# Attention phase: the finished batch's four tiles normalised on GpSimd, the new batch's four on ScalarE, one in a slot

## The chip, the cores and the metric

The kernel runs on one core of one Trainium2 chip. The time is the device time of one launch, in microseconds, median of several runs. The kernel is a whole two-layer network in one program of 39,953 instructions. The engines have queues of their own and are tied together by semaphores: TensorE (PE: matmuls and transposes, its weight loads shown as PEld), VectorE (DVE), ScalarE (ACT), GpSimd (POOL) and SyncE (SP, the DMAs).

## What is computed

The input is 16 batches of 512 rows of 128 numbers. The reference is a chain of six residual blocks; the change lies in the phase that computes the first three and prepares the fourth:

```python
x = x + 0.5 * L0_ffn(layernorm(x))     # sqrt((xn @ cos(..))**2 + (xn @ sin(..))**2)
x = x + L0_attn(layernorm(x))          # 16 heads, rotary, softmax(q k * scale) v, Wo
x = x + 0.5 * L0_ffn(layernorm(x))
x = x + 0.5 * L1_ffn(layernorm(x))     # top-2 counts of 8 experts over all rows
x = x + L1_attn(layernorm(x))          # a state-space mixer in chunks of 128
x = x + 0.5 * L1_ffn(layernorm(x))
```

`layernorm(x)` is `(x - mean) / sqrt(var + 1e-5)` over the 128 numbers of a row. The kernel computes it as `x * rstd + shift` with `shift = -mean * rstd`, one `rstd` and one `shift` for each row, so for each partition of a tile of 128 rows.

## The kernel before

**Three phases.** `attention_phase` runs first, to about 1617 us, then `mixer_phase` and `last_ffn_phase`. Each phase has its own semaphores and ends in a `sem_clear` on GpSimd and a barrier.

**Iterations and slots.** The attention phase has 19 iterations (`ITERATIONS = BATCH + 3`), and each has 64 slots (`SLOTS = NT * HEADS`). A slot is a place in the order in which each engine's queue is written: every engine's block has the loop `for i ... for q in range(SLOTS)`, and the table `ATTENTION_AT` says at which slot which step is issued. Within an engine, instructions run strictly in that order. Iteration i works on three batches at once: it takes in the *new* batch i (`is_new`, i up to 15), does attention for batch i - 2 (`is_att`, i from 2 to 17) and finishes the *old* batch i - 3 (`is_old`, i from 3). So iterations 3 to 15 have a new and an old batch ("mixed"), 0 to 2 only a new one, 16 to 18 only an old one; 18 has no attention.

**The attention inside a slot.** For each slot TensorE issues one matmul of shifted scores (`shifted_scores`, L708), which ScalarE turns into exponentials (`exponentials`, L506), and one matmul of plain scores for the next batch (`scores`, L724), of which VectorE takes the maximum (L347). The shifted scores go to one of two banks and wait for the exponential two before. Once in four slots TensorE issues `values` (L746), and once in eight `denominators` (L755). The latter read `prs`, the sums of two heads' exponentials, which GpSimd makes in `add_pair` (L579), four for each pair: those of heads 6 and 7 at slots 28 to 31, and the denominators that read them at slot 35. Exponentials of the next head but one overwrite the exponentials that were summed, and so wait for `prs` too (slots 32 to 35 for the pair of slots 28 to 31).

**The two laps.** Beside this, each iteration norms its tiles twice. Tiles 0 to 3 of `xn` belong to the new batch, 4 to 7 to the old one. Lap 1 (before the feed-forward block): statistics on VectorE at slots 5 and 6, aggregation at slot 8; `reciprocal_deviations` on GpSimd at slot 8 (L563 the power, L566 the shift); `normalise` on ScalarE at slots 11 to 14 (L468), a quarter of the iteration's tiles in each: two in a mixed iteration, one otherwise; `transposes` on TensorE at slot 16 (L634), the evacuation on ScalarE at 17 (L457), the feed-forward matmuls at 18 and 22 (L650), squares (L478) and their sums on GpSimd (L571), the root at 25 (L543), the residual on VectorE at 25 and 26 (L320). Lap 2 (before attention for the new batch, before the gate for the old one): statistics at 27 and 28, aggregation and deviations at 29, `normalise` at 31 to 34, transposes at 36, evacuation at 35 (behind the exponential of that slot), gate at 37 (L659), projections from 37 on (L665).

**Order on GpSimd in lap 2.** At slot 28 one sum of the pair, at slot 29 L563 and L566, then the sum of slot 29, then those of 30 and 31. The sums of slots 29 to 31 stand in the queue behind the deviations.

ScalarE's normalisation before:

```python
act.wait_ge(S["shift"], 2 * i + lap)
ts = tiles(i)
for t in ts[len(ts) // 4 * part:len(ts) // 4 * (part + 1)]:
    ins = a.activation(xn[:, t, :], src(t), ACT.Identity, scale=rstd[:, t:t + 1],
                       bias=shift[:, t:t + 1])
```

TensorE's transposes wait for one semaphore `xn`, which the last tile's normalisation raises. SyncE's queue (the loads of the next batch, the stacked queries and keys, the stores of the old batch) has no step at the edited place: its DMAs wait for `y_new`, `y_old`, `lo`, `st` and `mrow`.

Of the kernel before, what the change touches and what calls it, by code (L numbers as in the profile page):

```python
# [18 lines left out]
ALU = mybir.AluOpType  # L19
ACT = mybir.ActivationFunctionType  # L20
# [4 lines left out]
NT = SEQ // P  # L25
# [4 lines left out]
STK = 3 * DH + 1  # L30
W_SCALE = 64.0
ATT_SCALE = float((64 / 16) ** -0.5)


def rope_tables():
# [48 lines left out]
def attention_phase(nc, ins, x3_out, n3_out, w, cnt_acc, later):  # L84
# [4 lines left out]
    with ExitStack() as ctx:  # L89
        def sb(name, shape, dt=F32):  # L90
            return ctx.enter_context(nc.sbuf_tensor(name, shape, dt))

        x8 = sb("x8", [P, 8, D])
# [36 lines left out]

        ps = ctx.enter_context(nc.psum_tensor("ps", [P, 8, 512], F32))

        names = ("x_in", "var", "xn", "xT", "xnT", "ff", "sq", "ss", "h", "y_new", "y_old", "pair", "pair_free",
                 "rot", "hi", "lo", "gate", "gate_read", "st", "exp", "s", "s_read", "mrow", "rstd",
                 "pv", "den", "norm", "wo", "x2", "v", "dve", "x_out", "ones",
                 "xnh", "xnl", "v_ps", "prs", "dn", "dd", "o", "shift", "place_in", "n_out", "kept_hi", "kept_lo",
# [4 lines left out]
        for c in range(HEAD_GROUPS):  # L141
            S["stacked", c] = ctx.enter_context(nc.semaphore(f"a_stacked{c}"))
        nums = sorted(s.num for s in S.values())
        assert nums[-1] - nums[0] + 1 == len(nums)


        first, second = (pr[:, k].rearrange("p t n -> p (t n)") for k in range(2))
# [26 lines left out]
        def is_new(i):  # L174
            return i < BATCH
# [4 lines left out]
        def is_old(i):  # L180
            return 3 <= i
# [4 lines left out]
        def tiles(i):  # L186
            return [NT * h + t for h in halves(i) for t in range(NT)]
# [25 lines left out]
        with nc.Block(no_gpsimd_drain=True) as block:  # L213
# [234 lines left out]
            def _(act):  # L448
# [12 lines left out]
                            act.wait_ge(S["v_ps"], NT * (i - 1))  # L461
                        a.copy(xnh[:, i % 2], ps[:, 4, :]).then_inc(S["xnh"], 1)

                def normalise(i, src, lap, part):
                    act.wait_ge(S["shift"], 2 * i + lap)
                    ts = tiles(i)
                    for t in ts[len(ts) // 4 * part:len(ts) // 4 * (part + 1)]:
                        ins = a.activation(xn[:, t, :], src(t), ACT.Identity, scale=rstd[:, t:t + 1],  # L468
                                           bias=shift[:, t:t + 1])
                        if t == ts[-1]:  # L470
                            ins.then_inc(S["xn"], 1)

                def squares(i, k):
                    f = ffns_before(i) + k
# [36 lines left out]
                for i in range(ITERATIONS):  # L511
                    for q in range(SLOTS):
                        s, g = q // NG, q % NG
                        if is_att(i):
                            exponentials(i - 2, s, g)
                            if q in AT["values"]:
                                t = AT["values"].index(q)
                                act.wait_ge(S["v_ps"], NT * (i - 2) + t + 1)
                                a.copy(vt[:, t, :], ps[:, 5, :]).then_inc(S["v"], 1)
                            if s and s % NG == 0 and g == 3:  # L520
                                numerators(i - 2, s // NG - 1)
                        for part in range(4):
                            if q == AT["xn1"] + part:
                                normalise(i, lambda t: x8[:, t, :], 1, part)
                            if q == AT["xn2"] + part:
                                if part == 0:
                                    if is_new(i):
                                        act.wait_ge(S["y_new"], i + 1)
                                    if is_old(i):
                                        act.wait_ge(S["y_old"], i - 2)  # L530
                                normalise(i, lambda t: ynew[:, i % 4, t, :] if t < NT else yold[:, t - NT, :], 2, part)
                        if q == AT["evac1"]:
                            transposed(i, 1)
                        if q == AT["squares"]:
                            for k in range(2):
                                squares(i, k)
                        if q == AT["squares_b"]:
                            for k in range(2, len(tiles(i)) // 2):
                                squares(i, k)
                        if q == AT["sqrt"]:  # L540
                            a0, b0 = span(i)
                            act.wait_ge(S["ss"], ffns_before(i + 1))
                            a.activation(hh[:, a0:b0, :], hh[:, a0:b0, :], ACT.Sqrt, scale=0.25).then_inc(S["h"], 1)  # L543
                        if q == AT["evac2"]:
                            transposed(i, 2)
                        if is_old(i) and q == AT["next_hi"]:
                            act.wait_ge(S["xnT"], 2 * i + 2)
                            if i > 3:
                                act.wait_ge(S["n_out"], 16 * (i - 3))
                            a.copy(kept[:, 0], xnTo[:, :]).then_inc(S["kept_hi"], 1)  # L550
                        if is_new(i) and q in high_at:
                            high(i, high_at[q])
                    if is_att(i):
                        numerators(i - 2, NG - 1)

            @block.gpsimd
            def _(pool):
                g = nc.gpsimd

                def reciprocal_deviations(i, lap):  # L560
# [4 lines left out]
                    pool.wait_ge(S["rstd"], 2 * i + lap)  # L565
                    g.tensor_tensor(shift[:, a0:b0], nmean[:, a0:b0], rstd[:, a0:b0], ALU.mult).then_inc(S["shift"], 1)  # L566

                def add_squares(i, k):
                    pool.wait_ge(S["sq"], ffns_before(i) + k + 1)
                    t = tiles(i)[2 * k]  # L570
                    g.tensor_tensor(hh[:, t:t + 2, :], sq[:, k % 2, :, 0, :], sq[:, k % 2, :, 1, :],  # L571
                                    ALU.add).then_inc(S["ss"], 1)
# [19 lines left out]
                for i in range(ITERATIONS):  # L592
                    for q in range(SLOTS):
                        if q == AT["aggr1"]:
                            reciprocal_deviations(i, 1)
                        if q == AT["squares"]:
                            for k in range(2):
                                add_squares(i, k)
# [2 lines left out]
                                add_squares(i, k)  # L601
                        if q == AT["aggr2"]:
                            reciprocal_deviations(i, 2)
                        if is_old(i) and q == AT["next_lo"]:
                            pool.wait_ge(S["kept_hi"], i - 2)
                            g.tensor_tensor(kept[:, 1], xnTo[:, :], kept[:, 0], ALU.subtract).then_inc(S["kept_lo"], 1)
# [13 lines left out]
            def _(pe):  # L620
                mm = nc.tensor.matmul

                def transposes(i, lap):
                    pe.wait_ge(S["xn"], 2 * i + lap)
                    if lap == 1:
                        if is_att(i):
                            pe.wait_ge(S["v"], NT * (i - 1))
# [141 lines left out]
                for i in range(ITERATIONS):  # L769
# [33 lines left out]
                    if is_att(i):  # L803
                        values(i - 2, NG * NT - 1)
                        denominators_directly(i - 2, HEADS - 1)
        nc.gpsimd.sem_clear(range(nums[0], nums[-1] + 1))
        nc.all_engine_barrier(sem_only=True)


# [132 lines left out]
def mixer_phase(nc, x_in, n_in, x_out, n_out, w, ew, cnt_acc):  # L942
# [4 lines left out]
    with ExitStack() as ctx:  # L947
# [60 lines left out]
               "sqy": NT, "ms_mm": NT, "ms": 1, "rms": 1}  # L1008
        S = {n: ctx.enter_context(nc.semaphore("m_" + n)) for n in [*PER, "x_in0", "x_in1", "x_out0", "x_out1", "n_in0", "n_in1", "n_out", "dve", "pool", "start", "counted", "weights", "rate"]}
        nums = sorted(s.num for s in S.values())  # L1010
        assert nums[-1] - nums[0] + 1 == len(nums)

        AT = MIXER_AT
        SLOTS = 1 + max(max(a) if isinstance(a, tuple) else a for a in AT.values())
# [14 lines left out]
        with nc.Block(no_gpsimd_drain=True) as block:  # L1029
# [493 lines left out]
            def _(pe):  # L1523
# [144 lines left out]
                for i in range(ITERATIONS):  # L1668
                    ffn, prep, scan, tail = batches(i)
                    for q in range(SLOTS):  # L1670
# [55 lines left out]
                        if prep is not None:  # L1726
# [7 lines left out]
                                turn_bc(prep)  # L1734
                            if q == AT["scores"]:
                                scores(prep)
        nc.gpsimd.sem_clear(range(nums[0], nums[-1] + 1))
        nc.all_engine_barrier(sem_only=True)


def last_ffn_phase(nc, x_in, n_in, x_out, w, ew, cnt_acc):
# [4 lines left out]
    with ExitStack() as ctx:  # L1746
# [17 lines left out]
        for k in range(OUT):  # L1764
            S["x_out", k] = ctx.enter_context(nc.semaphore(f"f_x_out{k}"))
        nums = sorted(s.num for s in S.values())
        assert nums[-1] - nums[0] + 1 == len(nums)

        def upto(name, b, n):

# [5 lines left out]
        with nc.Block(no_gpsimd_drain=True) as block:  # L1776
# [139 lines left out]
            def _(pe):  # L1916
# [24 lines left out]
                for b in range(BATCH + 1):  # L1941
                    for e in range(EXPERTS):
                        if b < BATCH:
                            expert(b, e)
                        if e == 7 and b:
                            turn_sum(b - 1)
        nc.gpsimd.sem_clear(range(nums[0], nums[-1] + 1))
        nc.all_engine_barrier(sem_only=True)


# [45 lines left out]
```

## Time and profile before

| | |
|---|---|
| median of 3 runs | 2524.42 us |
| the runs | 2524.15, 2524.42, 2532.09 us |
| profiled execution: span | 2524.8 us |
| attention phase | to about 1617 us |
| iterations 3 to 15 | 229.06 to 1450.93 us |
| PE busy | 2163.5 us (86%) |
| DVE busy | 1827.8 us (72%) |
| POOL busy | 1455.5 us (58%) |
| ACT busy | 1410.7 us (56%) |

The span runs from the first instruction's start to the last one's end in the profiled execution; no time outside it is listed for that execution, so its own time is taken as the span of 2524.8 us, which is 0.4 us above the median. A row of a timeline has the start and the duration in us, the engine, the line, the operation, out<-in by the program's names, shapes, the number of instructions taken together, and in brackets how long the engine stood idle before it and what it waited for. `PEclk` is the share of full speed that TensorE's clock was granted.

### The profile page before, as it was taken

What the parts mean: (1) busy time and instruction counts of PE and PEld (TensorE: products, weight loads), DVE (VectorE), ACT (ScalarE), POOL (GpSimd) and SP (SyncE); (2) the same over time, 40 slices, a digit from 0 to 9 for tenths busy, and PEclk for the clock granted to TensorE, in tenths of its full rate; (3) what the DMA queues carried; (4) which work ended last, traced back from release to release, by engine and by line L of the source; (5) the groups of instructions that cost most, each with busy time, mean ns of one, the idle gap of its engine ahead of it and who ended that gap; (6) DMA issues with size and microseconds to landing.
All of it is one profiled execution on the core that took longest, in us unless ns stands there. A gap on an engine that the chain in (4) does not pass through costs nothing. (4 is left out here: it accounts for less than half of the span.)

```text
span 2524.8 us, 39953 instructions
## 1 busy us (share of the span) xinstructions
PE 2163.5 (86%) x14226; PEld 994.3 (39%) x14226; DVE 1827.8 (72%) x4240; ACT 1410.7 (56%) x2651; POOL 1455.5 (58%) x1264
## 2 busy tenths in 40 slices
PE   3689989989889889989989998569898899898878
PEld 1223333333323333323323322236566566665534
DVE  5777777777777777777777773358888888887668
ACT  2166566566566566566566566254555655556234
POOL 3366666665665665665665645146555656565358
PEclk9799999999999999999999999689999999999789
DMA  3221211112112112112112120100000000000033
GB/s 116 55 49 38 50 36 46 47 35 51 42 34 51 43 34 56 38 34 58 35 34 59 31 69 9 30 13 22 26 22 26 26 22 26 22 18 14 14 100 109
DMA packets 86598, 103.70 MB, mean 41 GB/s; under 512 B 10240, under 2 KB 68736, under 8 KB 86272
## 3 DMA queue, kind: packets, MB, share of 16 engines
q1 hardware_dynamic: 86400, 101.16, 15.3%
q8 instruction: 113, 1.85, 0.3%
q14 instruction: 85, 0.70, 0.1%
HBM read 29.55 MB, written 20.97 MB: 20 GB/s over the span
## 5 line engine op out<-in xcount | busy, mean ns | idle before, releaser
L347 DVE TENSOR_REDUCE mS<-ps 128x1 f32<-128x512 f32 x1024 | 676.9, 681 | 301.8 <-PE ps L724 297.3
L506 ACT ACTIVATE pr<-ps 128x512 f32<-128x512 f32 x1024 | 585.9, 597 | 383.7 <-PE ps L708 365.6
L579 POOL TENSOR_TENSOR prs<-pr 128x512 f32<-128x512 f32 x384 | 487.3, 1288 | 243.3 <-ACT pr L506 243.3
L708 PE MATMUL ps<-qst,kst 97*128 97x512 f16 x1024 | 397.2, 391 | 53.3 <-ACT pr L506 52.2
L724 PE MATMUL ps<-kst,qst 96*128 96x512 f16 x1024 | 400.4, 392 | 36.6 <-DVE mS L347 25.7
L746 PE MATMUL ps<-pr,vt 128*32 128x512 f32 x2048 | 279.6, 619 | 0.0
L708 PEld LDWEIGHTS ps<-qst,kst 97*128 97x128 f16 x1024 | 99.1, 98 | 419.3 <-ACT pr L506 307.3
L583 POOL TENSOR_TENSOR terms<-terms 128x512 f32<-128x512 f32 x128 | 162.4, 1268 | 69.3 <-DVE terms L340 69.3
L340 DVE TENSOR_TENSOR terms<-ps,shared 128x512 f32<-128x512 f32 x256 | 173.1, 678 | 34.9 <-POOL lo L588 29.7
L588 POOL TENSOR_TENSOR lo<-terms,hi 128x512 f16<-128x512 f32 x128 | 148.0, 1156 | 76.9 <-ACT hi L486 76.9
L724 PEld LDWEIGHTS ps<-kst,qst 96*128 96x128 f16 x1024 | 101.1, 99 | 150.4 <-DVE mS L347 80.1
L486 ACT CAST hi<-terms 128x512 f16<-128x512 f32 x128 | 78.8, 616 | 114.0 <-POOL terms L583 114.0
L755 PE MATMUL ps<-prs,ones 128*32 128x512 f32 x768 | 108.2, 637 | 33.9 <-POOL prs L579 33.9
L1394 ACT ACTIVATE m_sqy<-m_yzT 128x256 f32<-128x256 f32 x64 | 26.6, 415 | 179.3 <-DVE m_yzT L1205 179.2
L665 PE MATMUL ps<-xnh,wq 128*128 128x512 f16 x256 | 98.9, 390 | 31.3 <-DVE terms L340 22.4
L1491 POOL TENSOR_TENSOR m_own<-m_own 128x256 f32<-128x256 f32 x64 | 78.1, 1221 | 78.9 <-ACT m_own L1372 78.9
L1164 DVE TENSOR_TENSOR m_xv<-m_xr,m_coef 128x1536 f32<-128x1536 f32 x64 | 118.5, 1854 | 0.0
L1533 PE MATMUL m_ps<-m_xe,ew_hl 128*128 128x512 f16 x384 | 105.3, 395 | 9.8 <-DVE ew_hl L1240 4.2
L1486 POOL TENSOR_TENSOR m_rl<-m_rl 128x512 f32<-128x512 f32 x32 | 60.3, 1886 | 91.5 <-ACT m_rl L1398 91.5
L563 POOL TENSOR_TENSOR rstd<-veps,minus_half 128x8 f32<-128x8 f32 (+1 forms) x38 | 55.1, 1450 | 96.2 <-DVE veps L313 96.2
L665 PE MATMUL ps<-xnh,wk 128*128 128x512 f16 x256 | 97.2, 382 | 12.4 <-DVE terms L340 12.4
L571 POOL TENSOR_TENSOR xn<-sq 128x256 f32<-128x256 f32 x64 | 46.7, 749 | 100.4 <-ACT sq L478 100.3
(267 smaller groups left out, 4399.2 us busy)
## 6 DMA issues: line engine op xcount, KB each, us to landing
qst<-hi SPq DMA_DIRECT2D x128, 128.0 KB, 2.4
kst<-hi SPq DMA_DIRECT2D x128, 128.0 KB, 2.4
qst<-lo SPq DMA_DIRECT2D x64, 128.0 KB, 2.4
kst<-lo SPq DMA_DIRECT2D x64, 128.0 KB, 2.4
x<-in_q SPq DMA_DIRECT2D x16, 256.0 KB, 2.8
shared<-in_rope SPq DMA_DIRECT2D x1, 4096.0 KB, 14.4
x<-yold SPq DMA_DIRECT2D x16, 256.0 KB, 2.5
n<-kept SPq DMA_DIRECT2D x16, 256.0 KB, 2.1
```

Source lines behind the costliest of these rows:

```text
L340: v.tensor_tensor(terms[:, p % 2, c, :], ps[:, 4 + c, :], w["rope"][:, 2 * kq + c, g, :], ALU.mult).then_inc(S["pair_free"], 1)
L347: v.tensor_reduce(mS[:, b % 2, t, s:s + 1], ps[:, 2 + n % 2, :], AX, ALU.max).then_inc(S["s_read"], 1)
L506: a.activation(pr[:, s % 2, g, :], ps[:, g % 2, :], ACT.Exp, scale=ATT_SCALE).then_inc(S["exp"], 1)
L579: g.tensor_tensor(prs[:, c, :], pr[:, 0, c, :], pr[:, 1, c, :], ALU.add).then_inc(S["prs"], 1)
L583: g.tensor_tensor(terms[:, p % 2, 0, :], terms[:, p % 2, 0, :], terms[:, p % 2, 1, :], ALU.add).then_inc(S["rot"], 1)
L588: g.tensor_tensor(lo[:, p // NG, p % NG, :], terms[:, p % 2, 0, :], hi[:, p // NG, p % NG, :], ALU.subtract).then_inc(S["lo"], 1)
L665: ins = mm(out, lhs[a], rhs[b], start=k == 0, stop=k == 2)
L708: mm(ps[:, g % 2, :], kst[:, h, P * kt:P * kt + P], qst[:, h, :], start=True, stop=True).then_inc(S["st"], 1)
L724: mm(ps[:, 2 + n % 2, :], qst[0:3 * DH, h, P * t:P * t + P], kst[0:3 * DH, h, :], start=True, stop=True).then_inc(S["s"], 1)
L746: ins = mm(ps[DH * g:DH * g + DH, 6, :], vt[:, kt, DH * h:DH * h + DH], pr[:, s % 2, g, :], start=kt == 0, stop=kt == NT - 1, skip_group_c ...
L755: ins = mm(ps[DH * g:DH * g + DH, 7, :], w["ones"][:, 0:DH], prs[:, g, :], start=n % 2 == 0, stop=n % 2 == 1, skip_group_check=True)
L1164: v.tensor_tensor(xv[:, t % 2].rearrange("p c h r q -> p c h (r q)"), xr[:, b % 2, t].rearrange("p (o h) r q -> p o h (r q)", o=1).to_broa ...
```

## The change

The old batch's four tiles are normalised by GpSimd, at slot 8 for lap 1 and at slot 29 for lap 2, right behind the deviations. Each is one `tensor_scalar` with a multiplication and an addition, with two scalars for each partition; GpSimd waits first for its own shift to be complete. ScalarE keeps the new batch's four, one in each of slots 11 to 14 and 31 to 34, and nothing in iterations 16 to 18. A new semaphore `xn_old` counts GpSimd's part, and TensorE's transposes wait for `xn`, `xn_old` or both. Semaphore numbers need no longer be contiguous; at the end of each phase they are cleared in as many ranges as there are. In the new iterations 0 to 2 ScalarE's work is as before.

```diff
+def clear_semaphores(nc, nums):
+    first = nums[0]
+    for n, after in zip(nums, nums[1:] + [None]):
+        if after != n + 1:
+            nc.gpsimd.sem_clear(range(first, n + 1))
+            first = after
...
-                def normalise(i, src, lap, part):
+                def normalise(i, src, lap, t):
                     act.wait_ge(S["shift"], 2 * i + lap)
-                    ts = tiles(i)
-                    for t in ts[len(ts) // 4 * part:len(ts) // 4 * (part + 1)]:
-                        ins = a.activation(xn[:, t, :], src(t), ACT.Identity, scale=rstd[:, t:t + 1],
-                                           bias=shift[:, t:t + 1])
-                        if t == ts[-1]:
-                            ins.then_inc(S["xn"], 1)
+                    ins = a.activation(xn[:, t, :], src, ACT.Identity, scale=rstd[:, t:t + 1],
+                                       bias=shift[:, t:t + 1])
+                    if t == NT - 1:
+                        ins.then_inc(S["xn"], 1)
...
-                        for part in range(4):
-                            if q == AT["xn1"] + part:
-                                normalise(i, lambda t: x8[:, t, :], 1, part)
-                            if q == AT["xn2"] + part:
-                                if part == 0:
-                                    if is_new(i):
-                                        act.wait_ge(S["y_new"], i + 1)
-                                    if is_old(i):
-                                        act.wait_ge(S["y_old"], i - 2)
-                                normalise(i, lambda t: ynew[:, i % 4, t, :] if t < NT else yold[:, t - NT, :], 2, part)
+                        for t in range(NT):
+                            if is_new(i) and q == AT["xn1"] + t:
+                                normalise(i, x8[:, t, :], 1, t)
+                            if is_new(i) and q == AT["xn2"] + t:
+                                act.wait_ge(S["y_new"], i + 1)
+                                normalise(i, ynew[:, i % 4, t, :], 2, t)
...
+                def normalise_old(i, lap):
+                    b = i - 3
+                    if lap == 1:
+                        pool.wait_ge(S["xT"], 2 * i)
+                    else:
+                        pool.wait_ge(S["y_old"], b + 1)
+                    pool.wait_ge(S["shift"], 2 * i + lap)
+                    for t in range(NT, 2 * NT):
+                        src = x8[:, t, :] if lap == 1 else yold[:, t - NT, :]
+                        ins = g.tensor_scalar(xn[:, t, :], src, rstd[:, t:t + 1], shift[:, t:t + 1], ALU.mult, ALU.add)
+                    ins.then_inc(S["xn_old"], 1)
...
                         if q == AT["aggr1"]:
                             reciprocal_deviations(i, 1)
+                            if is_old(i):
+                                normalise_old(i, 1)
...
                         if q == AT["aggr2"]:
                             reciprocal_deviations(i, 2)
+                            if is_old(i):
+                                normalise_old(i, 2)
...
                 def transposes(i, lap):
-                    pe.wait_ge(S["xn"], 2 * i + lap)
+                    if is_new(i):
+                        pe.wait_ge(S["xn"], 2 * i + lap)
+                    if is_old(i):
+                        pe.wait_ge(S["xn_old"], 2 * (i - 3) + lap)
...
-        nc.gpsimd.sem_clear(range(nums[0], nums[-1] + 1))
+        clear_semaphores(nc, nums)
```

## Rows read from the trace of the kernel before

**Rows 1.** The page: busy time and share of the span, by engine.

```profile
PE 2163.5 (86%) x14226; PEld 994.3 (39%) x14226; DVE 1827.8 (72%) x4240; ACT 1410.7 (56%) x2651; POOL 1455.5 (58%) x1264
```

**Rows 2.** Iterations 3 to 15: us, busy (x) of PE, PEld, DVE, ACT, POOL; clock, DMA.

```profile
229.06:1450.93 1221.87, 1100.05 (x6188) 393.18 (x6188) 894.31 (x1995) 763.89 (x1417) 760.77 (x651) 0.98 0.18 43
```

**Rows 3.** Timeline of POOL: the deviations of lap 1, iterations 3, 9, 10, 16.

```profile
229.06 1.65 POOL L563 TENSOR_TENSOR rstd<-veps,minus_half 128x8 f32<-128x8 f32 x1 [0.88 <-DVE veps L313]
...
792.75 1.65 POOL L563 TENSOR_TENSOR rstd<-veps,minus_half 128x8 f32<-128x8 f32 x1 [0.87 <-DVE veps L313]
...
887.50 1.65 POOL L563 TENSOR_TENSOR rstd<-veps,minus_half 128x8 f32<-128x8 f32 x1 [0.88 <-DVE veps L313]
...
1450.93 1.02 POOL L563 TENSOR_TENSOR rstd<-veps,minus_half 128x4 f32<-128x4 f32 x1 [0.18 <-DVE veps L313]
```

**Rows 4.** Waits of PE in iterations 3 to 15: us, times, longest.

```profile
PE ps L708 <- ACT pr L506: 47.9, 78, 1.0
PE ps L755 <- POOL prs L579: 26.9, 38, 1.0
```

**Rows 5.** Timeline of ACT, iteration 8, lap 1: slots 11, 15 and 16.

```profile
701.57 0.88 ACT L468 ACTIVATE xn<-x,shift,rstd 128x128 f32<-128x128 f32 x2 [0.30 <-POOL shift L566]
...
706.09 1.06 ACT L506 ACTIVATE pr<-ps 128x512 f32<-128x512 f32 x2
```

**Rows 6.** Timeline of PE, iteration 8, lap 1: slot 14 and the transposes.

```profile
703.64 0.39 PE L708 MATMUL ps<-qst,kst 97*128 97x512 f16 x1
...
706.25 1.09 PE L634 MATMUL ps<-ident,xn 128*128 128x128 f32 x8 [0.16 <-ACT xn L468]
```

**Rows 7.** Timeline of POOL, iteration 8, lap 1.

```profile
701.33 0.20 POOL L566 TENSOR_TENSOR shift<-nmean,rstd 128x8 f32<-128x8 f32 x1
703.00 5.01 POOL L579 TENSOR_TENSOR prs<-pr 128x512 f32<-128x512 f32 x4 [1.47 <-ACT pr L506]
713.23 1.42 POOL L571 TENSOR_TENSOR xn<-sq 128x256 f32<-128x256 f32 x2 [5.21 <-ACT sq L478]
```

**Rows 8.** Timeline of POOL, iteration 8, lap 2.

```profile
727.74 1.65 POOL L563 TENSOR_TENSOR rstd<-veps,minus_half 128x8 f32<-128x8 f32 x1 [1.77 <-DVE veps L313]
729.47 0.20 POOL L566 TENSOR_TENSOR shift<-nmean,rstd 128x8 f32<-128x8 f32 x1
729.63 3.72 POOL L579 TENSOR_TENSOR prs<-pr 128x512 f32<-128x512 f32 x3
```

**Rows 9.** Timeline of PE, iteration 8, lap 2: slots 35 and 36.

```profile
732.45 0.39 PE L708 MATMUL ps<-qst,kst 97*128 97x512 f16 x1 [0.64 <-ACT pr L506]
...
733.41 1.07 PE L755 MATMUL ps<-prs,ones 128*32 128x512 f32 x8 [0.34 <-POOL prs L579]
...
734.85 1.04 PE L634 MATMUL ps<-ident,xn 128*128 128x128 f32 x8
```

**Rows 10.** Groups of POOL instructions with their shapes: busy us, mean ns, idle before.

```profile
L579 POOL TENSOR_TENSOR prs<-pr 128x512 f32<-128x512 f32 x384 | 487.3, 1288 | 243.3 <-ACT pr L506 243.3
...
L1455 POOL TENSOR_SCALAR m_nmean<-m_mv 128x4 f32<-128x4 f32 x32 | 7.3, 228 | 45.0 <-DVE m_veps L1073 45.0
```

**Rows 11.** Timeline of PE and POOL, lap 2 of iterations 16 and 17.

```profile
1479.94 1.06 PE L755 MATMUL ps<-prs,ones 128*32 128x512 f32 x8 [1.12 <-POOL prs L579]
...
1552.29 3.72 POOL L579 TENSOR_TENSOR prs<-pr 128x512 f32<-128x512 f32 x3
...
1556.49 1.31 PE L755 MATMUL ps<-prs,ones 128*32 128x512 f32 x8
```

**Rows 12.** Timeline of ACT and PE, lap 1 of iteration 18.

```profile
1596.31 1.65 ACT L468 ACTIVATE xn<-x,shift,rstd 128x128 f32<-128x128 f32 x4 [12.00 <-POOL shift L566]
...
1598.01 1.12 PE L634 MATMUL ps<-ident,xn 128*128 128x128 f32 x4 [5.43 <-ACT xn L468]
```

**Rows 13.** Busy times, clock, DMA (columns as Rows 2): lap 2 of iterations 9 and 10.

```profile
820.85:830.15 9.30, 6.82 (x30) 2.08 (x31) 4.39 (x7) 5.58 (x13) 5.52 (x5) 0.82 0.36 82
915.60:924.90 9.30, 7.61 (x47) 2.65 (x48) 5.21 (x9) 7.56 (x18) 5.52 (x5) 1.00 0.38 85
```

More of the change, by code:

```diff
@@ L131, in attention_phase @@
         ps = ctx.enter_context(nc.psum_tensor("ps", [P, 8, 512], F32))
-        names = ("x_in", "var", "xn", "xT", "xnT", "ff", "sq", "ss", "h", "y_new", "y_old", "pair", "pair_free",
+        names = ("x_in", "var", "xn", "xn_old", "xT", "xnT", "ff", "sq", "ss", "h", "y_new", "y_old", "pair", "pair_free",
                  "rot", "hi", "lo", "gate", "gate_read", "st", "exp", "s", "s_read", "mrow", "rstd",
@@ L143, in attention_phase @@
         nums = sorted(s.num for s in S.values())
-        assert nums[-1] - nums[0] + 1 == len(nums)
         first, second = (pr[:, k].rearrange("p t n -> p (t n)") for k in range(2))
@@ L1010, in mixer_phase @@
         nums = sorted(s.num for s in S.values())
-        assert nums[-1] - nums[0] + 1 == len(nums)
         AT = MIXER_AT
@@ L1736, in _ @@
                                 scores(prep)
-        nc.gpsimd.sem_clear(range(nums[0], nums[-1] + 1))
+        clear_semaphores(nc, nums)
         nc.all_engine_barrier(sem_only=True)
@@ L1766, in last_ffn_phase @@
         nums = sorted(s.num for s in S.values())
-        assert nums[-1] - nums[0] + 1 == len(nums)
         def upto(name, b, n):
@@ L1946, in _ @@
                             turn_sum(b - 1)
-        nc.gpsimd.sem_clear(range(nums[0], nums[-1] + 1))
+        clear_semaphores(nc, nums)
         nc.all_engine_barrier(sem_only=True)
```

## The prediction, made before the changed kernel was run

> **What bounds the kernel now.** First the page: TensorE is busy for 86% of the span, no other engine for over 72% [rows 1]. Then the stretch of the iterations that the change touches most, 3 to 15: 1221.87 us, TensorE 1100 of it, ScalarE 764, GpSimd 761 [rows 2]. So TensorE is the bound, and a gain or a loss there is what makes TensorE stand still. Third, whom it waits for: in these 13 iterations 47.9 us for an exponential of ScalarE and 26.9 us for a sum of GpSimd's (`add_pair`, L579) [rows 4]. Fourth, the timelines of both laps of iteration 8, engine by engine, to find which of these waits lies at the edited place. Last the repeat: lap 1's deviations (L563) mark each iteration's turn; iteration 9 lasts 94.75 us (792.75 to 887.50), and from 229.06 to 1450.93 there are 13 [rows 3].
>
> **Lap 1, slots 11 to 16.** ScalarE issues two normalisations (0.88 us) and one exponential in each of four slots [rows 5]. TensorE's shifted scores need the exponential two before, so they fall to ScalarE's pace, and the transposes of slot 16 start at 706.25 after a last wait for L468 [rows 6]. GpSimd has its shift at 701.53 and then nothing to do until 703.00 [rows 7].
>
> **Lap 2, slots 31 to 36.** ScalarE's pace is the same, but something else ends last. GpSimd's shift is done at 729.67, and three sums of a pair, held back behind it in GpSimd's queue, run from 729.63 to 733.35 [rows 8]. TensorE's denominators of slot 35 start at 733.41, after 0.34 us of waiting for just these, and the transposes come behind them in TensorE's queue at 734.85, with no wait for a normalisation [rows 9]. So lap 2 hangs on the chain variance, deviations, shift, three sums, denominators. In all 13 iterations the sums end 5.6 us behind the start of lap 2's L563, as here.
>
> **The price of one normalisation on GpSimd.** The trace has no such instruction: one input, a multiplication and an addition, two scalars from each partition, 128x128. Start to start, the two-input 128x512 sum takes (3.72 - 1.288) / 2 = 1.22 us [rows 8, 10] and the 128x256 one 1.42 / 2, some 0.69 us with the overlap [rows 7]. That is 2.07 ns for each column and 0.16 us fixed, so 0.43 us for a two-input instruction of 128 columns. The nearest below is the small TENSOR_SCALAR, 0.23 us long for four columns [rows 10], 0.19 from start to start. The ends are 0.19 and 0.43; a row of this length lies near the upper one, and two scalars must be fetched as well, so I take 0.40. Nothing in the rows excludes a dearer one; that is a rival.
>
> **What the change does, part by part.**
> 1. Lap 1, mixed iterations (13): four instructions of 484 ns leave ScalarE (half of rows 5's pairs). New walk: the normalisation of slot 11 still starts at 701.57. The exponential of slot 14 is now held by its scores, which TensorE issues at 703.64 behind `values` [rows 6]: plus 0.39 and a handover of 0.09 it starts at 704.12. The next instruction follows 0.48 behind [rows 5], so the last normalisation runs from 704.60 to 705.08 and the transposes start near 705.2 instead of 706.25: **-1.05 us**.
> 2. Lap 1 on GpSimd: shift done at 701.53, handover 0.08, four at 0.40: ready at 703.2, two microseconds ahead of the transposes. The sums behind them start at 703.2 instead of 703.00, and the first of them is read by the exponential that runs at 706.57 [rows 5, 7]. Cost nothing; that cover is gone if one instruction takes over 0.9 us.
> 3. Lap 2, mixed iterations: the four stand between the shift and the three sums. They wait for the shift to be complete (0.20 + 0.08 instead of 0.16 from start to start, +0.12) and take 1.60. The sums end 1.72 us later, at 735.07, and as GpSimd was already the one waited for, all of it goes to the denominators, and from there to the 36th scores, the transposes, the evacuations, gate and projections, all behind them in TensorE's queue: **+1.72 us**. Late next is ScalarE: its exponentials of slots 33 to 35 overwrite what the same sums read, so they wait too. What ScalarE saves in lap 2 is worth nothing.
> 4. Together +0.67 us an iteration, x13 = +8.7.
> 5. Iteration 16 (old only): lap 1 was paced by TensorE, nothing; lap 2 already waits 1.12 us for the sums, so +1.72. Iteration 17: the sums end at 1556.01, TensorE asks at 1556.49 [rows 11], a slack of 0.48, so +1.24. Iteration 18 has no attention: ScalarE's four take 1.65 us between shift and transposes [rows 12], GpSimd's 1.60: nothing. Sum +3.0.
> 6. Iterations 0 to 2: one tile a slot before and after, nothing. No DMA moves. One more semaphore, perhaps one more clear at the end of a phase: under 0.2 us.
> 7. **TensorE's clock.** In lap 2 of iteration 9 the granted clock averages 0.82 over 9.3 us: full level (2.4 GHz), then a stretch at half (1.2 GHz) just over the denominators and transposes; in iteration 10 it stays full [rows 13]. Seven of the 13 are like the first, six like the second. With x7 = 94.75, the six take (1221.87 - 663.25) / 6 = 93.10 us, so a drop here costs 1.65 us. What comes ahead of it is the thin stretch in which TensorE waits for exponentials and sums, and step 3 makes it 1.7 us thinner in all of them. The upper end is that all six fall too, 6 x 1.65 = +9.9; the lower is 0, as part of a low stretch would now lie over the wait. I take +5.0.
>
> Sum: 2524.8 + 8.7 + 3.0 + 5.0 = 2541.5. The span of the profile is 0.4 above the median of 2524.42, so 2541.
>
> **The rivals.**
> - **A cheap instruction.** If one input is read at half the time of two, it costs 0.16 + 0.13 = 0.29. Lap 2 loses 1.28, a mixed iteration 0.23, x13 = 3.0; iterations 16 and 17 +1.28 and +0.80; iteration 18 gains 0.45 a lap: +4.2, and with 5.0 for the clock 2534, without it 2529. For it speaks that the instruction reads one tensor. Chance 0.22. (The Trainium skill, GPSIMD Engine Reference, Engine selection, holds GpSimd to be about half VectorE's speed for two inputs but near its full rate for one; its side-by-side cycle accounting has 1.03 cycles an element at 1.2 GHz, an estimate of 0.11 us here, 0.27 with the fixed part. By that the sum without the clock would be about +3. No row here has such an instruction at length.)
> - **Not slower.** Lap 1's gain of 1.05 outweighs lap 2's loss once one instruction takes under (1.05 - 0.12) / 4 = 0.23 us. At the lower end, 0.19, an iteration gains 0.17 (x13 = -2.2), 16 and 17 lose 1.3, and 18 gains 1.8: 2522. Against it: 0.19 is the time of four columns. Chance 0.13.
> - **Faster.** The drops of the clock hang on where the thin stretch falls. If the shifted timing takes the seven away, at the cheap end, 2522 - 11.5 = 2511. The wait grows, which speaks against it. Chance 0.05.
> - **A dear instruction.** If the scalars cost like two more operands, 0.16 + 0.53 = 0.69: lap 2 +2.88, so 1.83 x 13 = 23.8, 16 and 17 +5.3, 18 +2.2, clock up to +9.9: 2566. Lap 1 stays covered. Chance 0.13.
> - The forecast (0.33 to 0.5 us each, 2532 to 2552) has 0.47.
>
> **Range and chances.** 0.3%, about what a measurement of this kernel can tell from no change, is 7.6 us: faster below 2516.8, slower above 2532.0. Same: "not slower" and a fourth of the cheap case, 0.19. Slower 0.76, faster 0.05. The range 2524 to 2560 leaves out most of the dear case, the faster one and part of "not slower".
>
> **What would show it.** Right: lap 2's denominators (L755) wait some 2 us for L579 instead of 0.34, and the sums end 7.3 us behind L563 instead of 5.6; lap 1's transposes start 3.9 us behind the shift (L566) instead of 4.9; the iterations last 93.8 us or 95.4, more of them the latter. Wrong: if the new instruction's start-to-start time is not 0.3 to 0.5 us, the size falls; if the denominators of slot 35 wait for something else or don't move, the mechanism does.

## The result, and the profile after

The changed kernel takes 2553.77 us (median of 4 runs, 2549.37 to 2555.06) against 2524.28 us of the kernel before: ratio 1.0088, 95% interval 1.0063 to 1.0113. The two medians by themselves are 29.5 us or 1.2% apart, just outside that interval; a second series of runs (e9, below) gave 1.0101 (1.0085 to 1.0116). So it is slower, by some 0.9 to 1.2%. The profiled execution took 2552.72 us with a span of 2550.7, 25.9 more than the span before. The time of a profiled execution is thus 2.0 us above its span, and 1.8 to 2.2 us in all the runs below, where the section on the time before took the two as equal.

The page's first part, against [rows 1]:

```profile
PE 2162.3 (85%) x14226; PEld 996.4 (39%) x14226; DVE 1827.3 (72%) x4240; ACT 1368.4 (54%) x2523; POOL 1508.6 (59%) x1392
```

ScalarE lost 42 us of work and GpSimd gained 53, and TensorE, the bound, has the same work in a longer span: it stands still more. Iterations 3 to 15 now run from 229.72 to 1474.71 us, 1244.99 us against 1221.87 of [rows 2] (columns as there):

```profile
229.72:1474.71 1244.99, 1099.03 (x6188) 396.69 (x6188) 892.99 (x1995) 730.57 (x1313) 804.71 (x755) 0.98 0.18 42
```

In the attention phase the span grew by 29.8 us in all (23.1 of it in these 13 iterations, 4.4 in iteration 16, 1.1 in 17); the mixer took 4.2 us less than in the profile before, with the same number of instructions on every engine and a mean granted clock of 0.96 instead of 0.95. One execution differs from the next by a few us: in the profile of e9, the same kernel, these 13 iterations take 1242.6 us, 20.7 over the kernel before.

**The new instruction.** The group of GpSimd's normalisations of lap 1, with shape, count, busy us and mean ns; lap 2's reads the same:

```profile
L578 POOL TENSOR_SCALAR xn<-x,rstd,shift 128x128 f32<-128x128 f32 x64 | 27.8, 448 | 2.8 <-POOL shift L567 2.8
```

27.8 us busy for 64 is 0.434 us of GpSimd's time for each. One is 448 ns long, and in a group of four the next starts 0.43 us after the one before.

**Lap 1** of iteration 8, GpSimd, ScalarE and TensorE, to be read beside [rows 5 to 7]:

```profile
710.49 0.20 POOL L567 TENSOR_TENSOR shift<-nmean,rstd 128x8 f32<-128x8 f32 x1
710.87 1.74 POOL L578 TENSOR_SCALAR xn<-x,rstd,shift 128x128 f32<-128x128 f32 x4 [0.18 <-POOL shift L567]
712.57 4.96 POOL L592 TENSOR_TENSOR prs<-pr 128x512 f32<-128x512 f32 x4
```

```profile
710.73 0.49 ACT L473 ACTIVATE xn<-x,shift,rstd 128x128 f32<-128x128 f32 x1 [0.31 <-POOL shift L567]
711.31 0.60 ACT L511 ACTIVATE pr<-ps 128x512 f32<-128x512 f32 x1
...
713.71 0.48 ACT L473 ACTIVATE xn<-x,shift,rstd 128x128 f32<-128x128 f32 x1
714.10 1.07 ACT L511 ACTIVATE pr<-ps 128x512 f32<-128x512 f32 x2
```

```profile
713.87 0.39 PE L728 MATMUL ps<-qst,kst 97*128 97x512 f16 x1
...
714.55 1.06 PE L654 MATMUL ps<-ident,xn 128*128 128x128 f32 x8
```

ScalarE issues one normalisation between exponentials, the last from 713.71. The transposes start 4.06 us behind the shift (L567, L566 before) where it was 4.92; counted from L564 (L563 before) it is 5.78 us here, 5.64 in most iterations, and was 6.64. GpSimd's tiles are there two microseconds sooner.

**Lap 2** of the same iteration, GpSimd and TensorE, beside [rows 8, 9]:

```profile
736.01 1.65 POOL L564 TENSOR_TENSOR rstd<-veps,minus_half 128x8 f32<-128x8 f32 x1 [1.76 <-DVE veps L320]
737.74 0.20 POOL L567 TENSOR_TENSOR shift<-nmean,rstd 128x8 f32<-128x8 f32 x1
738.12 1.73 POOL L578 TENSOR_SCALAR xn<-yold,rstd,shift 128x128 f32<-128x128 f32 x4 [0.18 <-POOL shift L567]
739.82 3.70 POOL L592 TENSOR_TENSOR prs<-pr 128x512 f32<-128x512 f32 x3
```

```profile
739.07 0.39 PE L728 MATMUL ps<-qst,kst 97*128 97x512 f16 x1 [0.51 <-ACT pr L511]
...
741.76 0.39 PE L728 MATMUL ps<-qst,kst 97*128 97x512 f16 x1 [2.09 <-ACT pr L511]
...
743.57 1.93 PE L775 MATMUL ps<-prs,ones 128*32 128x512 f32 x8 [1.20 <-POOL prs L592]
...
746.26 1.30 PE L654 MATMUL ps<-ident,xn 128*128 128x128 f32 x8
```

The four stand between L567 and the sums (L592). The sums end at 743.52, 7.51 us behind L564, where it was 5.61, and the denominators (L775) start at once behind them, after 1.20 us of waiting (0.34 before). The forecast had "some 2 us" of waiting at this place. The rest of the delay lies one slot ahead, where the scores wait 2.09 us for an exponential that itself waits for the sums. Their eight matmuls then last 1.93 us instead of 1.07, and the transposes come at 746.26, 10.25 us behind L564, where it was 7.11. ScalarE waits for the same sums:

```profile
741.11 0.60 ACT L511 ACTIVATE pr<-ps 128x512 f32<-128x512 f32 x1 [1.72 <-POOL prs L592]
...
742.33 0.60 ACT L511 ACTIVATE pr<-ps 128x512 f32<-128x512 f32 x1 [0.24 <-POOL prs L592]
```

**TensorE's clock** over lap 2 of iterations 8 and 9 (columns as [rows 2]), against [rows 13]:

```profile
736.90:746.20 9.30, 5.51 (x25) 1.04 (x24) 2.80 (x5) 4.38 (x9) 6.36 (x9) 0.85 0.26 59
832.50:841.80 9.30, 5.50 (x25) 1.06 (x25) 2.71 (x5) 4.38 (x9) 6.28 (x9) 0.85 0.26 59
```

Both are below full. A stretch at half level over slots 35 and 36, called a drop below, stands in all 13 iterations of the changed kernel and in seven of the kernel before. In iteration 8 the level is half (1.2 GHz) from 743.37 to 746.78, right over the denominators, the scores behind them and the start of the transposes.

### The profile page after: what moved, and what is told of

It reads as the page before. It is cut to its first block and busy times, and to the rows that moved or that the text cites. A ratio compares the mean times of both kernels' runs of the same rounds, so it can differ in the third digit from the quotient of the medians.

```text
span 2550.7 us, 40042 instructions
## 1 busy us (share of the span) xinstructions
PE 2162.3 (85%) x14226; PEld 996.4 (39%) x14226; DVE 1827.3 (72%) x4240; ACT 1368.4 (54%) x2523; POOL 1508.6 (59%) x1392
## 5 line engine op out<-in xcount | busy, mean ns | idle before, releaser
L592 POOL TENSOR_TENSOR prs<-pr 128x512 f32<-128x512 f32 x384 | 486.4, 1288 | 223.6 <-ACT pr L511 223.6
L775 PE MATMUL ps<-prs,ones 128*32 128x512 f32 x768 | 115.1, 674 | 45.4 <-POOL prs L592 45.4
L685 PE MATMUL ps<-xnh,wq 128*128 128x512 f16 x256 | 100.0, 395 | 29.9 <-DVE terms L347 21.2
L564 POOL TENSOR_TENSOR rstd<-veps,minus_half 128x8 f32<-128x8 f32 (+1 forms) x38 | 55.1, 1450 | 95.1 <-DVE veps L320 95.1
```

The lines of the kernel that those rows point to most:

```text
L592: g.tensor_tensor(prs[:, c, :], pr[:, 0, c, :], pr[:, 1, c, :], ALU.add).then_inc(S["prs"], 1)
L685: ins = mm(out, lhs[a], rhs[b], start=k == 0, stop=k == 2)
L775: ins = mm(ps[DH * g:DH * g + DH, 7, :], w["ones"][:, 0:DH], prs[:, g, :], start=n % 2 == 0, stop=n % 2 == 1, skip_group_check=True)
```

## The experiments

The theory: what is lost is the sums' place in GpSimd's queue in lap 2, plus a drop of the clock that follows the longer wait; lap 1 is a gain. The rivals: GpSimd's work as such disturbs the others (1); lap 1's gain is given back later (2); the old tiles themselves come too late (3); the clock's drops are hidden or come anyway (4). A fifth, for e7's gain, comes up in e10. The runs were taken in series, each with its own runs of the kernel before (medians 2527.45 us for e1 to e4, 2527.47 for e5 to e8, 2530.14 for e9 to e11), and a ratio is against those.

**e1: lap 1 alone moved.**

```diff
                         if q == AT["aggr2"]:
                             reciprocal_deviations(i, 2)
-                            if is_old(i):
-                                normalise_old(i, 2)
```

with ScalarE's lap 2 as before the change, two tiles a slot.

> GpSimd normalises the old tiles in lap 1 only; lap 2 is ScalarE's as before the change. Theory (the loss is lap 2's queue on GpSimd, lap 1 is a gain): lap 1's transposes keep their 5.64 us behind L563 (6.64 before), lap 2's denominators are back at 5.66 us behind it, every iteration from 3 to 15 is 1.0 us shorter than before the change, 92.1 or 93.8 us by whether the clock falls: about 2511 us, from 2503 to 2520 by how often it falls. Rival 1 (GpSimd's instructions as such disturb VectorE or the clock, in either lap): slower than 2524. Rival 2 (lap 1's gain is not real, only moved to a later wait): 2524.

Measured: 2506.64 us, ratio 0.9917 (0.9904 to 0.9929) to the kernel before. Lap 2 of its iteration 8:

```profile
721.15 3.71 POOL L604 TENSOR_TENSOR prs<-pr 128x512 f32<-128x512 f32 x3
```

```profile
724.92 1.06 PE L787 MATMUL ps<-prs,ones 128*32 128x512 f32 x8 [0.34 <-POOL prs L604]
...
726.36 1.04 PE L666 MATMUL ps<-ident,xn 128*128 128x128 f32 x8
```

The denominators are back at 5.65 us behind the deviations, with the old 0.34 us of waiting, the iterations last 92.1 us, and rival 2 falls, and rival 1 for lap 1: with this lap moved the kernel is faster than before. Its 13 iterations are 21.7 us shorter, 13 of them forecast. The rest goes with the clock, which has the drop in one of the 13 iterations only, though lap 2 and its waits are as before the change.

**e2: lap 2 alone moved**, the mirror image (ScalarE's lap 1 two tiles a slot, GpSimd's four only in lap 2).

> GpSimd normalises the old tiles in lap 2 only; lap 1 is ScalarE's as before the change. Theory: the denominators of slot 35 stay at 7.56 us behind L563, lap 1's transposes go back to 6.64, iterations last 96.5 us each with the clock's drop: 2553.8 + 13 x 1.0 = 2567 us. Rival 2 (lap 1's gain is given back later anyway): 2554.

Measured: 2575.05 us, ratio 1.0189 (1.0173 to 1.0204). Transposes of lap 1 at 6.65 us, denominators of lap 2 at 7.6, as expected; the iterations last 96.6 or 97.8 us by turns. The second kind, seven of the 13, has a stretch at half level twice as long (34.7 to 41.5 us into the iteration instead of 35.8 to 39.2) and is 1.1 us longer each time, which is about the 8 us above the expectation; the kernel before was also 3.2 us higher in this series than in the first.

**e3: lap 2's four behind the sums.**

```diff
                         if q == AT["aggr2"]:
                             reciprocal_deviations(i, 2)
-                            if is_old(i):
-                                normalise_old(i, 2)
+                        if is_old(i) and q == AT["aggr2"] + 3:
+                            normalise_old(i, 2)
```

> As the changed kernel, but in lap 2 GpSimd issues its four normalisations at slot 32, behind the three sums, not between the shift and the sums. Theory (the sums' lateness is the loss): the denominators are back at 5.66 us behind L563; the tiles are ready at 5.6 + 1.75 = 7.4, the transposes at 7.45 instead of 7.10 before the change, so lap 2 costs 0.35 and lap 1 gains 1.0: some 13 x 0.65 = 8.5 us under the kernel before, 2516, from 2506 to 2524 by the clock. Rival 3 (what is late is the old tiles themselves, for the transposes): these come 3.7 us later than in the changed kernel, so slower than it, 2554 + 13 x 2 = 2580 or more.

Measured: 2513.99 us, ratio 0.9944 (0.993 to 0.9958). Lap 2 of iteration 9:

```profile
814.08 1.65 POOL L564 TENSOR_TENSOR rstd<-veps,minus_half 128x8 f32<-128x8 f32 x1 [1.77 <-DVE veps L320]
...
815.96 3.71 POOL L592 TENSOR_TENSOR prs<-pr 128x512 f32<-128x512 f32 x3
819.67 1.73 POOL L578 TENSOR_SCALAR xn<-yold,rstd,shift 128x128 f32<-128x128 f32 x4
```

```profile
819.73 1.07 PE L775 MATMUL ps<-prs,ones 128*32 128x512 f32 x8 [0.59 <-POOL prs L592]
...
821.50 1.06 PE L654 MATMUL ps<-ident,xn 128*128 128x128 f32 x8 [0.16 <-issue]
```

The denominators stand 5.65 us behind L564, the transposes at 7.42, 0.10 us behind the end of the last tile (821.40), which is 3.5 us later than in the changed kernel. Three of the 13 iterations have the drop. The kernel is 40 us faster than the changed one with the same instructions on the same engines. Rival 3 falls, and rival 1 for lap 2, and the place in the queue is the cause.

**e4: TensorE kept at work during the wait.**

```diff
+                        if is_att(i) and is_old(i) and is_new(i) and q in (34, 35):
+                            if q == 34:
+                                pe.wait_ge(S["sq"], ffns_before(i + 1))
+                            for _ in range(5):
+                                mm(ps[:, 4, :], kst[0:3 * DH, NG * ring(i - 2, 2), 0:P], qst[0:3 * DH, NG * ring(i - 2, 2), :],
+                                   start=True, stop=True)
```

> As the changed kernel, with five extra matmuls (96x128 by 96x512, f16, into a bank that the transposes overwrite) at slot 34 and five at slot 35 of iterations 3 to 15, in TensorE's idle time ahead of the denominators: 1.1 us each five. Theory: the sums still end 7.5 us behind L563, but the clock no longer falls to half there, and the transposes come at 9.0 us instead of 10.25; 1.65 us less in each iteration: 2553.8 - 13 x 1.65 = 2532 us, or 2529 with what iterations 3, 14 and 15 lost more. Rival 4 (the low clock is hidden by the waits, or it comes whatever TensorE does): 2554, or more by the extra matmuls.

Measured: 2533.48 us, ratio 1.0027 (1.0007 to 1.0046), so 20 us under the changed kernel with ten matmuls more an iteration. Its ten runs spread more than the others', from 2524 to 2547 us. Iteration 8:

```profile
733.97 1.06 PE L775 MATMUL ps<-prs,ones 128*32 128x512 f32 x8
...
735.41 1.04 PE L654 MATMUL ps<-ident,xn 128*128 128x128 f32 x8
```

The denominators wait for the sums as before (7.57 us behind L564) but last 1.06 us instead of 1.93, and the transposes come at 9.01 instead of 10.25. No iteration from 3 to 15 has the drop; iteration 16, which has no filler, has a stretch at half level from 30.2 to 37.0 us. An iteration lasts 94.0 us against 95.55: the drop cost 1.55. Rival 4 falls for the changed kernel.

**e5: the four twice in lap 2**, first into a spare tile, then the real ones.

```diff
+                    if lap == 2 and i < BATCH:
+                        for t in range(NT, 2 * NT):
+                            src = x8[:, t, :] if lap == 1 else yold[:, t - NT, :]
+                            g.tensor_scalar(spare[:, t - NT, :], src, rstd[:, t:t + 1], shift[:, t:t + 1], ALU.mult, ALU.add)
```

> As the changed kernel, but in lap 2 of iterations 3 to 15 GpSimd issues the four normalisations a second time, into a spare tile, ahead of the real ones: 1.74 us more in the same place. Theory (the queue on GpSimd is passed on in full): the denominators at 9.3 us behind L563 instead of 7.56, iterations 97.3 us, 2553.8 + 13 x 1.74 = 2576 us, up to 2590 if the clock's low stretch grows with the wait. Rival 3 (some other fixed wait is what costs): well under 2570.

Measured: 2583.71 us, ratio 1.0231 (1.0216 to 1.0246). Denominators at 9.28 us, 1.72 later: passed on in full. Most iterations are 1.7 to 3.2 us longer than the usual 95.55. The stretch at half level grew too, to 6.8 or 13.7 us in all 13; where it lies from 32.8 us on, largely over the wait, the iteration is 1.7 us longer and no more.

**e6: the same filler in the kernel before**, three matmuls at each of the two slots.

> The kernel before the change with three extra matmuls each (96x128 by 96x512, f16) at slots 34 and 35 of iterations 3 to 15, in TensorE's idle time. Theory (the drop of the clock over slots 35 and 36 follows from the thin stretch ahead of it, in the kernel before in seven of 13 iterations): the clock stays full there in all 13, 7 x 1.65 = 11.5 us less, 2 us more for what of the matmuls doesn't fit: 2515 us. Rival 4 (the drops come whatever TensorE does): 2526.

Measured: 2530.41 us, ratio 1.0026 (1.0011 to 1.0041): no gain, as rival 4 has it, but not for its reason. In iteration 7 the low level now comes 30.1 us into the iteration and lasts 6.8 us, over the filler itself, which at half level no longer fits the gaps: the denominators start 7.85 us behind L563, with no wait, instead of 5.65:

```profile
635.88 1.49 PE L784 MATMUL ps<-qst,kst 96*128 96x512 f16 x3
637.30 1.49 PE L755 MATMUL ps<-prs,ones 128*32 128x512 f32 x8
```

Three of the 13 iterations are like this; in five a shorter stretch, from about 29.1 to 29.9 us on, puts the denominators at 6.2 to 6.6, and in the other five they stand at 5.9. The filler moved the drop forward in place of removing it. It settles nothing on what the drops of the kernel before cost. The profiled execution took 2525.58 us; five of the twelve runs took 2539 to 2542, and what they lost is not seen.

**e7: the sum of slot 29 first**, on top of e3.

```diff
-                        if q == AT["aggr2"]:
+                        if q == AT["aggr2"] + 1:
                             reciprocal_deviations(i, 2)
```

Slot 29's sum stands in the queue ahead of slot 30's entries, so it now runs while GpSimd waits for the variance.

> As e3_behind_sums, and lap 2's deviations (L563, L566) one slot later on GpSimd, behind the sum of slot 29, which then runs while GpSimd waits for the variance. Theory (lap 2 hangs on the chain deviations, three sums, denominators): only two sums are left behind the shift, they end at 4.4 us behind L563, the denominators come at 4.45, the old tiles are ready at 6.15, the transposes at 6.2 instead of 7.43: a further 1.2 us an iteration, 91.2 us each, some 2499 us. If ScalarE's or TensorE's own pace ends first, half of that: 2506.

Measured: 2490.95 us, ratio 0.9852 (0.9838 to 0.9867), the fastest version of this study. Lap 2 of iteration 9:

```profile
802.69 2.50 POOL L592 TENSOR_TENSOR prs<-pr 128x512 f32<-128x512 f32 x2 [3.31 <-ACT pr L511]
805.73 1.65 POOL L564 TENSOR_TENSOR rstd<-veps,minus_half 128x8 f32<-128x8 f32 x1 [0.55 <-DVE veps L320]
...
807.62 2.49 POOL L592 TENSOR_TENSOR prs<-pr 128x512 f32<-128x512 f32 x2
810.10 1.75 POOL L578 TENSOR_SCALAR xn<-yold,rstd,shift 128x128 f32<-128x128 f32 x4
```

```profile
810.20 1.06 PE L775 MATMUL ps<-prs,ones 128*32 128x512 f32 x8
...
811.95 1.06 PE L654 MATMUL ps<-ident,xn 128*128 128x128 f32 x8
```

Denominators 4.47 us behind L564, transposes at 6.21, iterations of 91.25 us. The transposes now follow GpSimd's last tile, which ends at 811.85, and ScalarE's relief in lap 2 is worth something (against e10). The time is 8 us under the expected 2499: the 13 iterations are 19.0 us shorter than e3's, 15.6 by the forecast's 1.2 each, and the three drops of e3 are gone.

**e8: the four twice in lap 1**, on top of e1.

> As e1_lap1_only, but in lap 1 of iterations 3 to 15 GpSimd issues the four normalisations twice, first into a spare tile: 1.74 us more ahead of the sums of slots 12 to 15. Theory (lap 1's cover is two microseconds wide): the tiles are ready at 3.7 us behind the shift, just ahead of the transposes at 3.9, which stay; but the first two sums end 0.9 us too late for the exponentials of slots 16 and 17, ahead of the evacuation: 0.5 to 0.9 us an iteration, 2513 to 2518 us. Rival 1 (any such work on GpSimd is passed on in full): 2506.6 + 13 x 1.74 = 2529.

Measured: 2528.48 us, ratio 1.0004 (0.9995 to 1.0013), above the expectation and at rival 1's 2529. The iterations tell it from the theory. Lap 1 of iteration 10:

```profile
891.50 1.75 POOL L592 TENSOR_SCALAR spare<-x,rstd,shift 128x128 f32<-128x128 f32 x4 [0.18 <-POOL shift L580]
893.23 1.75 POOL L595 TENSOR_SCALAR xn<-x,rstd,shift 128x128 f32<-128x128 f32 x4
894.94 4.95 POOL L609 TENSOR_TENSOR prs<-pr 128x512 f32<-128x512 f32 x4
```

```profile
896.29 0.60 ACT L521 ACTIVATE pr<-ps 128x512 f32<-128x512 f32 x1 [0.98 <-POOL prs L609]
897.48 0.60 ACT L521 ACTIVATE pr<-ps 128x512 f32<-128x512 f32 x1 [0.59 <-POOL prs L609]
```

The tiles are ready for the transposes, which stay (5.69 us behind L577), but the exponentials of slots 16 and 17 wait 0.98 and 0.59 us for the sums, and with them the evacuation. Lap 2 begins 28.18 us into the iteration instead of 27.09: 1.09 us lost, of 1.74 added, so it is not passed on in full. That is 14 of the 22 us, and the rest goes with the clock: seven iterations of 13 have the drop and are 94.7 to 94.8 us long, the others 93.2. That the time met rival 1's is chance.

**e9: the changed kernel again.**

> The changed kernel once more, unchanged, beside more runs of the kernel before on one chip: what the ratio is, and whether the clock falls in lap 2 of all 13 iterations again. Expected 2554 us, against 2524 to 2528 before: 1.009 to 1.012.

Measured: 2555.14 us, ratio 1.0101 (1.0085 to 1.0116). The transposes of lap 2 come 9.99 to 10.55 us behind the deviations in all 13 iterations, so the drop is there in each.

**e10: the order alone**, in the kernel before (the diff of e7).

> The kernel before the change, with lap 2's deviations one slot later on GpSimd, behind the sum of slot 29; ScalarE still normalises all eight tiles. Theory: the sums no longer end last, ScalarE's two normalisations a slot do: its last one ends 6.7 us behind L563, the transposes come at 6.75 instead of 7.10, and 0.35 us an iteration is gained, 2524.3 - 4.5 = 2520 us. Rival 5 (e7's gain is all the order's, nothing of it GpSimd's tiles): 1.2 us an iteration, 2509.

Measured: 2518.76 us, ratio 0.9959 (0.9945 to 0.9973). Nine iterations last 92.8 us, transposes at 6.73. Lap 2 of iteration 8, ScalarE and TensorE:

```profile
726.05 0.87 ACT L468 ACTIVATE xn<-yold,shift,rstd 128x128 f32<-128x128 f32 x2
```

```profile
725.50 1.07 PE L755 MATMUL ps<-prs,ones 128*32 128x512 f32 x8
...
726.98 1.09 PE L634 MATMUL ps<-ident,xn 128*128 128x128 f32 x8
```

As expected, ScalarE's two tiles a slot end last there (726.92, the transposes at 726.98), and rival 5 falls: the order alone moves the transposes by 0.38 us, against the 1.21 from e3 to e7 with GpSimd's tiles. It falls by these places, not by the time, which at 0.41% is more than twice the 4.5 us expected: the 13 iterations are 9.1 us shorter than before, some 4 by the 0.3 each, the rest with the drop in four of them instead of seven.

**e11: sum first, the four still ahead of the other two.**

> The changed kernel with lap 2's deviations one slot later on GpSimd, behind the sum of slot 29; the four normalisations still stand right behind the shift, ahead of the two sums that are left. Theory: the sums end 6.3 us behind L563, the denominators at 6.35, the transposes at 7.8 (9.0 with the clock at half): between 92.8 and 94.4 us an iteration, 2520 to 2540 us. Against e7_sum_first it is the place alone that differs: 1.9 us later denominators.

Measured: 2535.71 us, ratio 1.0029 (1.0014 to 1.0045), in ten runs from 2528 to 2550, with the profile from one of the shortest (2529.63). Lap 2 of iteration 8:

```profile
730.66 1.74 POOL L578 TENSOR_SCALAR xn<-yold,rstd,shift 128x128 f32<-128x128 f32 x4 [0.18 <-POOL shift L567]
732.36 2.48 POOL L592 TENSOR_TENSOR prs<-pr 128x512 f32<-128x512 f32 x2
```

```profile
734.90 1.06 PE L775 MATMUL ps<-prs,ones 128*32 128x512 f32 x8 [1.36 <-POOL prs L592]
```

Denominators at 6.34, transposes at 7.79 where the clock holds. Seven of the iterations last 94.4 to 96.5 us, with the drop, where e7 has none. Against e7 the place of four instructions costs 45 us, that stretch included.

## Why the prediction was right, point by point

- **What bounds each lap: right.** Lap 2 hung on deviations, sums, denominators before (e3, e10 show it by moving the queue alone), and lap 1 on ScalarE's pace.
- **The price of one instruction**, taken as 0.40 us, is 0.43: at the upper end, the two-input line's. Reading one tensor did not make it cheaper, so the rival of a cheap instruction fell, and with it what the Trainium skill's page GPSIMD Engine Reference (Engine selection, and Elementwise — side-by-side cycle accounting) would give: by "1-input is roughly line-rate" and 1.03 cycles an element I had estimated 0.27, and the trace shows 0.43, so page and measurement differ here.
- **Step 1**, -1.05 us: measured -0.98 to -1.00 in 12 iterations of 13 (5.64 to 5.66 against 6.64 us) and -0.86 in iteration 8.
- **Step 2**, lap 1 covered on GpSimd: right, the sums of slots 12 to 15 start at 712.57 and delay nobody. That the cover lasts to 0.9 us an instruction was wrong: e8, with 0.87 in effect, loses 1.09 us. The 0.9 was counted to the exponential at 706.57 of the kernel before, which step 1 itself moves 1.05 us forward. In the changed kernel this exponential runs from about 714.58 and the first sum ends at 713.86, so some 0.7 us are left over the 1.74, and the cover is gone at about 0.6 us an instruction (an estimate from these rows, which fits e8: 1.74 - 0.7 = 1.0). The rival of a dear instruction, at 0.69, would have lost some of lap 1's gain too.
- **Step 3**, +1.72: measured +1.90 (7.56 against 5.66). From the first of the four to the first sum are 1.70 us (738.12 to 739.82), and the wait for the shift cost 0.22 and not 0.12: 0.38 from the shift's start to the next instruction's, where it was 0.16. "What ScalarE saves in lap 2 is worth nothing" holds in this order only (e7).
- **Step 4**, +0.67 an iteration: +0.90 by the two measured parts, 11.7 us over 13 in place of 8.7.
- **Step 5**, +1.72 and +1.24: iterations 16 and 17 took 4.4 and 1.1 more. In 16 the denominators moved by 1.90, and the rest goes with a stretch at half level from 29.8 to 36.6 us that it did not have before. In 17 the denominators came 1.48 later, and lap 1's transposes 0.41 sooner (4.82 us against 5.23), a gain that the forecast left out. Iteration 18 lost 0.4 at its two transposes, against nothing forecast.
- **Step 7, the clock: right in kind, and half its size.** I took +5.0, halfway between none and all six of the iterations that had been spared. All six fell (+9.9), and 1.5 us of the 23.1 are left over, with iterations 3, 14 and 15 above these terms by 2.4 us and the others 0.9 below. These 6.4 us, the 3.0 of step 4, the 2.7 of iteration 16 and 1.0 at the ends of the phase lead from the forecast of +16.7 to the attention phase's +29.8. The other two phases gave back 3.9, hence 25.9 between the spans. Between the medians it is 29.5, because the profiled execution before lay about 2.5 us above its median (2524.8 and 2.0 against 2524.28) and the one after 1.1 below. The term that was mis-sized most is the choice of the middle for the clock. e4 shows for the changed kernel that the drop follows from the idle time ahead of it. In the four profiles where TensorE mostly waits 2.1 us or more at one go there (the changed kernel, e9, e2, e5) every one of the 13 iterations has it, so the upper end was the likelier one. That the time still fell into the range is owed to the range's width, 36 us, more than to this term.
- The rivals "not slower", "faster" and "a dear instruction" did not occur.

What stays open is why the kernel before and e8 had the drop in just seven of their 13 iterations and e1 in one, with the same waits in lap 2 (0.91 or less, 0.64 and 0.34 us): where in an iteration the level changes shifts from one to the next, and no run here set it. Since each drop moves the time by some 1.6 us, a run's time alone proves no single part of the sum; the places within the iteration do. Why the mixer gave back 4.2 us in the one profile is open too; in the second profile of the same kernel (e9) it took 799.2 us, in the first 796.2, and before 800.4.

## What to carry to other kernels

Before work is moved to an idle engine, look at what stands behind it in that engine's queue and who waits for that: here moving four instructions of 0.43 us gained 1.0 us an iteration in one place and cost 1.9 in the other, while the engine was idle for some 40% of the span in both. The same instructions behind the urgent ones, and one urgent one pulled ahead of a wait, turned +1% into -1.5%. When TensorE's wait grows, count the drop of its clock behind it at its full price if such a drop is already seen behind the shorter wait.

## What the runs showed of the hardware that was not expected

- GpSimd's one-input multiply-add with two scalars from each partition takes 448 ns at 128x128 f32 (429 from start to start), about what its two-input sum would by the rate and the fixed part read from [rows 7, 8, 10] (2.07 ns a column and 0.16 us).
- A few matmuls in the gaps kept TensorE's clock at full in one kernel (e4, -1.55 us an iteration) and in another (e6) moved the drop onto themselves in some iterations, with no gain in time: such a filler has to be measured.
